# First node stage with only the two powers on GpSimd, and interaction's relu rows and normalising a turn later

## What is computed

```python
h = x @ W
msg = h[src] * norm[src, None]
agg = segment_sum(msg, dst) * norm[:, None]
l2 = sqrt(sum(agg * agg, axis=1, keepdims=True))
out = tanh(agg / maximum(l2, 1e-12))
```

## Time and profile before

| | us |
|---|---|
| time, median of 3 runs | 4420.27 (4418.27 to 4423.72) |
| profiled execution | 4440.37 |
| its span | 4438.7 |

### The profile page before, as it was taken

How to read it: one execution, slowest core, us unless ns; L and a number is a source line. 1 busy time by engine, 2 the same in 40 slices (tenths; PEclk the granted TensorE clock), 3 DMA queues, 4 the chain that set the end, 5 groups by cost and what they waited for, 6 DMA issues and landing times. The chain is left out here.

```text
span 4438.7 us, 67467 instructions
## 1 busy us (share of the span) xinstructions
PE 3028.4 (68%) x12342; PEld 1728.7 (39%) x12342; DVE 3396.4 (77%) x9927; ACT 2153.8 (49%) x5600; POOL 2094.9 (47%) x2258
## 2 busy tenths in 40 slices
PE   5956644444445999478999224888886999706886
PEld 1255533333332444123444112555553666503443
DVE  6978858888886888675555685888884666697997
ACT  0057756776662222162222355766664666504554
POOL 0057767777774555006553002555544555203566
PEclk9967767677767999788999555989887999958998
DMA  2079967767773222174222496444444565503332
GB/s 51 2 210 285 286 207 230 230 223 228 230 225 89 64 62 61 40 229 86 60 62 47 131 245 164 116 118 122 118 120 131 196 200 194 170 0 112 113 112 87
DMA packets 621013, 627.71 MB, mean 141 GB/s; under 512 B 167332, under 2 KB 494590, under 8 KB 614468
## 3 DMA queue, kind: packets, MB, share of 16 engines
q1 hardware_dynamic: 572900, 523.78, 39.4%
q0 software_dynamic: 48000, 102.76, 9.6%
HBM read 333.97 MB, written 296.91 MB: 142 GB/s over the span
## 5 line engine op out<-in xcount | busy, mean ns | idle before, releaser
L1410 PE MATMUL r_pM<-r_masked,wr 128*128 128x512 f32 x1600 | 750.0, 622 | 55.2 <-DVE r_masked L1361 31.5
L1361 DVE SCALAR_TENSOR_TENSOR r_masked<-r_typ,r_hT 128x512 f32<-128x512 f32 x800 | 493.8, 689 | 241.4 <-ACT r_hT L1388 164.0
L1410 PEld LDWEIGHTS r_pM<-r_masked,wr 128*128 128x128 f32 x1600 | 308.7, 199 | 426.7 <-issue 326.1
L1252 PE MATMUL e_pY<-ident,e_agg 128*128 128x128 f32 x400 | 134.0, 438 | 370.3 <-issue 246.7
L741 POOL DMA_INDIRECT q_rows<-nr,row_x x200 | 258.0, 1290 | 209.4 <-PE q_pT L590 149.8
L2431 POOL DMA_INDIRECT out<-o_base,o_at_o x200 | 241.6, 1208 | 162.1 <-DVE o_base L2472 93.8
L741 POOL DMA_INDIRECT r_xs<-h_tab,r_at_s x200 | 216.1, 1080 | 87.7 <-issue 51.8
L741 POOL DMA_INDIRECT r_xs<-tab,r_at_s x200 | 214.1, 1071 | 89.1 <-issue 52.3
L1252 PEld LDWEIGHTS e_pY<-ident,e_agg 128*128 128x128 f32 x400 | 106.9, 327 | 382.3 <-issue 305.1
L590 PE MATMUL g_pT<-ident,g_hT 128*128 128x128 f32 x400 | 96.0, 384 | 226.5 <-ACT g_hT L1792 177.1
L1006 PE MATMUL na_pZ<-w,na_aT 128*128 128x128 f32 x784 | 159.6, 386 | 117.7 <-ACT na_aT L988 117.6
(11 more groups left out here) (418 smaller groups left out, 9048.8 us busy)
## 6 DMA issues: line engine op xcount, KB each, us to landing
xz<-na_xz SPq DMA_DIRECT2D x49, 1040.0 KB
r_typ<-vec_s SPq DMA_DIRECT2D x100, 256.0 KB
g_al<-alpha_s SPq DMA_DIRECT2D x100, 256.0 KB, 3.9
na_xz<-in_x SPq DMA_DIRECT2D x49, 512.0 KB
tab<-na_x SPq DMA_DIRECT2D x49, 512.0 KB
e_xin<-tab SPq DMA_DIRECT2D x49, 512.0 KB
hr<-e_hh SPq DMA_DIRECT2D x49, 512.0 KB
zh_s<-e_zh SPq DMA_DIRECT2D x49, 512.0 KB
```

The lines of the kernel that those rows point to most:

```text
L1252: pe.matmul(pY[s][:, cols], agg[s][:, cols], g.ident[:, :], start=True, stop=False)
L1361: v.scalar_tensor_tensor(masked[:, r, :], typ[d.slot(4)][:, :], float(r), hT[d.slot(2)][:, :], ALU.is_equal, ALU.mult).then_inc(ev.mk, 1)
L1410: pe.matmul(pM[s][:, :], g.wr[:, layer * R_ + r, :], masked[:, r, :], start=(r == 0), stop=(r == R_ - 1)).then_inc(ev.mm, 1)
```

## The change

In `node_rows` GpSimd keeps the two powers. The seven small steps around them become five instructions of DVE: `ve` = variance + eps behind the statistics (t-2); `q` = min(`rq`, 1e12) x norm of pair t-5, put behind `ve` and ahead of `y`; `bw` ahead of the product L946 (t-3), which waits for it; `part` = (`ss` + 1e-30) x norm and `tq` = `part` x norm ahead of the sum (t-4). `ve`, `rs`, `tq` and `rq` have two buffers and an event each.

In `interaction` the line is one turn longer. On DVE `nm` (now block t-5) and the normalising (t-6) move ahead of the message products. On ACT the relu rows (now t-5) move ahead of the copy `ws`. PE's transposes of `n_`, ACT's `ndT` and `att` and PE's matmul between them go from t-6 to t-7, SP's stores of `n_` and of `ndT` and `att` one turn later each; the store of `base` stays at t-6 and is now ahead of that of `n_`.

```diff
         @block.gpsimd
         def _(pool):
-            braid.credit(pool, ev.bw, ev.q)
-            c = Chain(pool, s_p, 8 * SLOTS, g)
+            braid.credit(pool, ev.rs, ev.rq)
...
                 p = pair(2)
                 if p:
-                    s, norm = p.slot(2), xz[p.slot(SLOTS)][:, :, INFO_AT]
-                    wait_alone(g, pool, ev.st, p.one())
-                    inverse_root(rs[:, :], mv[s][:, :, 1], EPS_LN)
-                    wait_alone(g, pool, ev.zr, p.back(2))
-                    c.step(pool.tensor_tensor(bw[s][:, :], rs[:, :], norm, ALU.mult))
-                    pool.sem_inc(ev.bw, 1)
+                    s = p.slot(2)
+                    wait_alone(g, pool, ev.bw, p.one_back(2))
+                    wait_alone(g, pool, ev.ve, p.one())
+                    pool.tensor_tensor(rs[s][:, :], ve[s][:, :], half[:, :], ALU.pow).then_inc(ev.rs, 1)
                 p = pair(4)
                 if p:
-                    s, norm = p.slot(2), xz[p.slot(SLOTS)][:, :, INFO_AT]
-                    c.step(pool.tensor_tensor(n2[:, :], norm, norm, ALU.mult))
-                    wait_alone(g, pool, ev.ss, p.now())
-                    wait_alone(g, pool, ev.r2, p.back(2))
-                    c.step(pool.tensor_tensor(q[s][:, :], ss[s][:, :], n2[:, :], ALU.mult))
-                    inverse_root(q[s][:, :], q[s][:, :], 1e-30)
-                    c.step(pool.tensor_scalar(q[s][:, :], q[s][:, :], 1e12, None, ALU.min))
-                    pool.tensor_tensor(q[s][:, :], q[s][:, :], norm, ALU.mult).then_inc(ev.q, 1)
+                    s = p.slot(2)
+                    wait_alone(g, pool, ev.q, p.one_back(2))
+                    wait_alone(g, pool, ev.tq, p.one())
+                    pool.tensor_tensor(rq[s][:, :], tq[s][:, :], half[:, :], ALU.pow).then_inc(ev.rq, 1)
...
         @block.vector
...
                     v.wait_ge(ev.st, p.one())
+                    v.wait_ge(ev.rs, p.one_back(2))
+                    v.tensor_scalar(ve[s][:, :], mv[s][:, :, 1], EPS_LN, None, ALU.add).then_inc(ev.ve, 1)
+                d = pair(5)
+                if d:
+                    v.wait_ge(ev.rq, d.one())
+                    v.wait_ge(ev.r2, d.back(2))
+                    v.scalar_tensor_tensor(q[d.slot(2)][:, :], rq[d.slot(2)][:, :], 1e12, xz[d.slot(SLOTS)][:, :, INFO_AT], ALU.min, ALU.mult).then_inc(ev.q, 1)
+                if p:
                     for m in MEMBERS:
...
                 p = pair(3)
                 if p:
                     s, rows = p.slot(2), xz[p.slot(SLOTS)]
+                    v.wait_ge(ev.rs, p.one())
+                    v.wait_ge(ev.zr, p.back(2))
+                    v.tensor_tensor(bw[s][:, :], rs[s][:, :], rows[:, :, INFO_AT], ALU.mult).then_inc(ev.bw, 1)
                     v.wait_ge(ev.bw, p.one())
...
+                p = pair(4)
+                if p:
+                    s, norm = p.slot(2), xz[p.slot(SLOTS)][:, :, INFO_AT]
+                    v.wait_ge(ev.ss, p.now())
+                    c.step(v.scalar_tensor_tensor(part[:, :], ss[s][:, :], 1e-30, norm, ALU.add, ALU.mult))
+                    v.wait_ge(ev.rq, p.one_back(2))
+                    v.tensor_tensor(tq[s][:, :], part[:, :], norm, ALU.mult).then_inc(ev.tq, 1)
...
                 p = pair(4)
                 if p:
                     s, rows = p.slot(2), xz[p.slot(SLOTS)]
-                    a.wait_ge(ev.q, p.one_back(2))
+                    a.wait_ge(ev.tq, p.one_back(2))
...
 def interaction(nc, g):
...
-    line = Line(4, 10, 7)
+    line = Line(4, 10, 8)
...
         @block.vector
...
+                b = at(5)
+                if b:
+                    v.wait_ge(ev.rz, b.now())
+                    v.wait_ge(ev.hh, b.back(1))
+                    v.scalar_tensor_tensor(nm[:, :], mv[:, :, 0], -1.0, rz[:, :], ALU.mult, ALU.mult).then_inc(ev.nm, 1)
+                d = at(6)
+                if d:
+                    s = d.slot(2)
+                    v.wait_ge(ev.rh, d.now())
+                    v.wait_ge(ev.ts, d.back(2))
+                    if d.k >= 2:
+                        v.wait_ge(w_n[s], 16 * d.uses(2))
+                    normalise(v, hh[s], mvh, rh, n_[s], ev.nn)
                 b = at(3)
...
         @block.scalar
...
+                d = at(5)
+                if d:
+                    s = d.slot(2)
+                    a.wait_ge(ev.nm, d.now())
+                    a.wait_ge(ev.nn, d.back(2))
+                    a.wait_ge(ev.ba, d.back(2))
+                    for j in range(J):
+                        last = a.activation(hh[s][:, j, :], x3[s][:, j, :], ACT.Relu, scale=rz[:, j:j + 1], bias=nm[:, j:j + 1])
+                    last.then_inc(ev.hh, 1)
+                if b:
                     a.wait_ge(ev.ww, b.now())
...
             def turn(at):
-                f = at(6)
+                f = at(7)
```

More of the change, by code:

```diff
@@ L838, in node_rows @@
     ctx = ExitStack()
-    names = "st bw ya t1 e1 yy zr ss q r2 x1".split()
+    names = "st ve rs bw ya t1 e1 yy zr ss tq rq q r2 x1".split()
     ev = events(g, "na_", names)
-    s_v, s_p, s_c = g.sem("na_v"), g.sem("na_p"), g.sem("na_c")
+    s_v, s_c = g.sem("na_v"), g.sem("na_c")
     l_x, w_x = ([g.sem(f"na_{n}{k}") for k in range(SLOTS)] for n in ("lx", "wx"))
@@ L851, in node_rows @@
         mv = some("mv", 2, [P, 2 * J, 2])
-        bw, ss, q = (some(n, 2, [P, 2 * J]) for n in ("bw", "ss", "q"))
-        rs, n2 = (sb(n, [P, 2 * J]) for n in ("rs", "nsq"))
+        ve, rs, bw, ss, tq, rq, q = (some(n, 2, [P, 2 * J]) for n in ("ve", "rs", "bw", "ss", "tq", "rq", "q"))
+        part = sb("part", [P, 2 * J])
         half = sb("half", [P, 2 * J])
@@ L892, in _ @@
         def _(pool):
-            braid.credit(pool, ev.bw, ev.q)
-            c = Chain(pool, s_p, 8 * SLOTS, g)
+            braid.credit(pool, ev.rs, ev.rq)
             pool.memset(half[:, :], -0.5).then_inc(s_c, 1)
             pool.wait_ge(s_c, 1)
-            def inverse_root(dest, values, floor):
-                c.step(pool.tensor_scalar(dest, values, floor, None, ALU.add))
-                c.step(pool.tensor_tensor(dest, dest, half[:, :], ALU.pow))
             def turn(pair, _):
@@ L904, in turn @@
                 if p:
[L905 to L910 removed]
+                    s = p.slot(2)
+                    wait_alone(g, pool, ev.bw, p.one_back(2))
+                    wait_alone(g, pool, ev.ve, p.one())
+                    pool.tensor_tensor(rs[s][:, :], ve[s][:, :], half[:, :], ALU.pow).then_inc(ev.rs, 1)
                 p = pair(4)
                 if p:
[L913 to L921 removed]
+                    s = p.slot(2)
+                    wait_alone(g, pool, ev.q, p.one_back(2))
+                    wait_alone(g, pool, ev.tq, p.one())
+                    pool.tensor_tensor(rq[s][:, :], tq[s][:, :], half[:, :], ALU.pow).then_inc(ev.rq, 1)
+            braid.sweep(pool, turn)
         @block.vector
         def _(v):
[L925 removed]
+            braid.credit(v, ev.st, ev.ve, ev.bw, ev.tq, ev.q)
             braid.credit_pairs(v, ev.ya, ev.zr, ev.x1)
[L927 removed]
+            c = Chain(v, s_v, 2 * SLOTS)
             def turn(pair, _):
@@ L1876, in turn @@
                     s = b.slot(2)
-                    wait_alone(g, sp, ev.nn, b.now())
-                    sp.dma_start(b.edge_rows(g.nr, N), n_[s][:, :, :]).then_inc(w_n[s], 16)
                     wait_alone(g, sp, ev.ba, b.now())
@@ L1881, in turn @@
                 b = at(7)
+                if b:
+                    s = b.slot(2)
+                    wait_alone(g, sp, ev.nn, b.now())
+                    sp.dma_start(b.edge_rows(g.nr, N), n_[s][:, :, :]).then_inc(w_n[s], 16)
+                b = at(8)
                 if b:
@@ L1981, in turn @@
                     stats(v, c, g, hh[d.slot(2)], sth, mvh, ev.sh)
-                if b:
-                    v.wait_ge(ev.rz, b.now())
-                    v.wait_ge(ev.hh, b.back(1))
-                    v.scalar_tensor_tensor(nm[:, :], mv[:, :, 0], -1.0, rz[:, :], ALU.mult, ALU.mult).then_inc(ev.nm, 1)
-                if d:
-                    s = d.slot(2)
-                    v.wait_ge(ev.rh, d.now())
-                    v.wait_ge(ev.ts, d.back(2))
-                    if d.k >= 2:
-                        v.wait_ge(w_n[s], 16 * d.uses(2))
-                    normalise(v, hh[s], mvh, rh, n_[s], ev.nn)
             line.sweep(v, turn, c)
@@ L2006, in turn @@
                     a.activation(a8T[:, :], pW[0:NSC, :], ACT.Copy).then_inc(ev.ac, 1)
-                b = at(6)
+                b = at(7)
                 if b:
@@ L2053, in turn @@
                     rstd(a, g, c, mvh, rh, ev.rh)
-                if b:
-                    s = b.slot(2)
-                    a.wait_ge(ev.nm, b.now())
-                    a.wait_ge(ev.nn, b.back(2))
-                    a.wait_ge(ev.ba, b.back(2))
-                    for j in range(J):
-                        last = a.activation(hh[s][:, j, :], x3[s][:, j, :], ACT.Relu, scale=rz[:, j:j + 1], bias=nm[:, j:j + 1])
```

(1 more changed line is left out.)

1 line of the change is left out of this document (removed).

## The result

The changed kernel takes 4404.5 us (median of 6 runs, 4402.4 to 4407.8) where the kernel before takes 4419.3 (6 runs, 4414.5 to 4428.8): a ratio of 0.9963 with a 95% interval of 0.995 to 0.9976, 15 us less. The forecast was 24 us less. The sign and the range held, but the way there was another: one stage gained twice what I said, and a stage whose code wasn't touched lost most of it again.

What follows compares the result with a forecast made beforehand. The prediction took GpSimd's chain to bound the node stage and DVE's order the interaction stage. Terms of -16 us (node) and -8 us (interaction) made -24 us, from 4420.3 to 4396 us, range 4376 to 4430.

Steps and rivals of the forecast that it cites:

- GpSimd's chain bounds the node stage, and DVE is next: Node stage: GpSimd's chain on itself sets the 7.47 us turn; after the change DVE sets it at 7.15 us.
- The size of DVE's additions: Node stage: five new DVE instructions add 0.7 to 1.3 us to 6.2, taken as 0.95; 14 us gained over 45 turns.
- The DMA engines as the next bound, at 7.1 us a turn: Node stage: one turn's four transfers take about 7.1 us at the present rate, next behind GpSimd's chain.
- The rival in which the transfers take over at 7.4 us: Node stage gains only 3 us and interaction 3, as PE's ring takes its gain back: 4414 us, chance 0.17.
- The power holds the port: Node stage rival: DVE's `y` and sum would stand behind GpSimd's powers; chance 0.02.
- Interaction, what goes: Interaction: DVE's stops ahead of `nm` and `n_`, PE's wait for `n_` and L1955's 12 stops go; scan waits for `pL`.
- the ring of 10.85 us and 0.5 for L1959: Interaction: PE's answer closes a 10.85 us ring; GpSimd's addition holds L1959 for 0.5 us, giving an 11.35 us undisturbed turn.
- The rival by which `base` also holds the last product: Interaction: L1959 and the last product both held, 11.85 us turn, half clock as often as now; 4435 us, chance 0.13.
- ten turns at half clock: Interaction: ten turns with PE at half clock, each 2.4 us above the 11.35 us turn.
- My -8 us for the stage: Interaction: +2 us from turns and slow turns, -3 behind slow ones, -7 where L1959 is not held; ends -35 and +25.
- The change touches these two alone: Whole kernel: only the node stage (383 us) and interaction (627 us) of the 4438.7 us span are touched.
- Carrying the profile's difference over to the median: Whole kernel: the profiled execution is 20 us above the timed median; the -24 us was applied to 4420.3.

Runs made afterwards that it cites:

- node_load: The changed kernel with the 36 looped node-stage turns loading only half the rows of x; its node stage took 351 us, in one profiled execution.
- a_mm: The changed kernel with GpSimd's two interaction sums waiting each turn until DVE has written message tile m; ratio 0.9911 to the kernel before.
- best: The changed kernel with GpSimd's interaction sums behind m and 94 idle DVE instructions ahead of the layer0_edges loop; 4342.8 us, ratio 0.983 to the kernel before.
- inter_only: The change's interaction with the node stage of the kernel before; ratio 0.9982 to the kernel before, 8 us less.
- a_pad94: The changed kernel with 94 idle DVE instructions ahead of the layer0_edges loop; ratio 0.9912 to the kernel before.

## Why the prediction was right or wrong

- **GpSimd's chain bounds the node stage, and DVE is next:** right. GpSimd waits for DVE ahead of both powers, and the idle time ahead of DVE's sum is gone, and the stage lasts 351.1 to 351.4 us in every profile that has it unaltered.
- **The size of DVE's additions:** the term of the sum that was mis-sized. I took 0.95 us for five operations; they take 0.75 in the turn shown and 0.77 in the mean. `ve` and `q` move what follows by 0.2 us, not the up to 0.36 that I allowed for their waits, which was an estimate without a row; `bw` and the wait behind it cost 0.2, not the 0.32 to 0.39 I had. Only `part` to `tq` to the sum was as thought, 0.37. The occupation before them was a little below 6.2 as well: 6.86 - 0.75 = 6.1. So the turn is 6.9 us, my low bound, and outside the 7.0 to 7.3 that I named as the sign. 45 x (7.47 - 6.9) = 26 us by my way of counting, 27.6 measured between the `y` rows, where I had 14; the last turns gave 3.5 where I had 2. The profile shows no stop of DVE for any of the new waits.
- **The DMA engines as the next bound, at 7.1 us a turn:** wrong. I read the busy share of the DMA engines, 0.93 before, as the time that the transfers need. The same transfers ran at 298 GB/s after and 273 before, in turns of 6.9 us, and node_load shows that they were not the limit even there. The rival in which the transfers take over at 7.4 us is out by the same rows.
- **The power holds the port (chance 0.02):** out. By it `y` and the sum would have stood behind GpSimd's powers, as L1955 stood behind the addition of 1.26 us; they don't. What the two engines share, no run shows. The `y` pair at 404.48, with both inputs in SBUF, takes its usual 1.30 us, though a power runs from 404.65 for 2.02 us and its second half begins inside that. But the power itself got longer, from 1.67 us to mostly 1.9 to 2.1; no run shows why.
- **Interaction, what goes:** right. L1955's stops are gone, as are the waits for `rz` and `rh`, and the scan waits for `pL`.
- **Interaction, the ring of 10.85 us and 0.5 for L1959:** right in kind and nearly in size. The hold is 0.585 us in the mean of the 50 turns, and without it a_mm and best run at a median turn of 10.6, 0.3 below my 10.85. With the hold the median is 11.35, the number of the forecast. The rival by which `base` also holds the last product came true in part: by 0.07 us a turn here, by 0.3 to 0.4 on the other chips, and never with a mean turn of 12.3.
- **Interaction, ten turns at half clock:** too many. The half clock itself is measured: PEclk 0.50 from 3016 to 3022 us of the kernel before, in the turn of rows 9. Two of 49 turns in the changed kernel exceed 12.5 us, against 13 before; over all profiles it is 1 to 5 with the change and 11 to 17 without. The granted clock of the stage rose from 0.85 to 0.91. I took the new gap ahead of the message transposes to be as harmful as the old ones, for which I had no row. My -8 us for the stage agree with the timed inter_only, but in the profiles the stage lost 10 to 22 us: I deducted 7 us for turns without a hold, of which the first profile has only three, and charged 24 us for ten slow turns where two came. In the profile these didn't cancel (553 us from first to last `nm`, where my terms give 570); that the timed 8 us are my 8 is luck.
- **"The change touches these two alone":** wrong, and the step that cost most. Everything outside the two stages was put at nothing because its instructions were the same. Their place wasn't. Without what layer0_edges lost, 28 us in the mean of the profiles, the change would have been worth 0.9%, 39 us (a_pad94, 0.9912), near the low end of my range at 4380. The missing term, 28 us or more slower, covered up the undersized one, 15 us too small: that the time fell into my own range is luck.
- **Carrying the profile's difference over to the median:** right for the timed result, but the two first profiles were no pair in gat_rows (498 and 483 us, where the same code has 483 on one chip and 492 to 498 on two others), which only became visible with more profiles.

## What to carry to other kernels

162 more instructions of DVE ahead of a loop of 326 slowed that loop down by 28 us with nothing in it changed: after a change, compare the untouched stages first, and look for waits on "issue" that recur once a trip (here nine of 2.9 to 4.1 us) together with more packets on the instruction queue (here 50 instead of 11). If they are there, idle instructions in a place where the engine waits anyway are a quick way to find a better place. Before moving work under GpSimd's sums of 128x512, list which DVE operations there have two SBUF operands (here one took 1133 ns instead of 548), and tie the sums to an event behind which DVE reads PSUM or one operand: in a_mm the stage took 580 instead of 611 us, and the statistics of `x3` (L567, one operand), over half of which start inside a sum there, took 277 ns in the median and 300 at most.

## What the runs showed of the hardware

- A DVE loop of 326 instructions took 28 us more on average in ten trips when it started at place 30 modulo 128 instead of 124: nine stops of 2.9 to 4.1 us, each with one packet of the instruction queue that starts 0.9 to 2.2 us into it, and 50 to 52 such packets from 700 to 1250 us instead of 7 to 11.
- GpSimd's addition of 128x512 held DVE's 128x384 product with two SBUF inputs for 0.585 us on average (1133 against 548 ns), as it held L1955 before. In inter_only the product took 1.03 to 1.59 us in the 25 turns in which it started inside such a sum, and 0.55 in the 25 others. The product from PSUM right behind it took 544 ns with the sum `base` beside it.
- Small operations (128x8) on DVE moved what follows by 0.08 to 0.2 us each in the turn shown, five of them by 0.77 in the mean of a turn, though each is shown with 0.16 or 0.17.
- A DMA share of 1.00 at 298 GB/s was not a bound: with an eighth of the bytes gone (0.88, 271 GB/s) the stage took the same 351 us.
